# Four samples written out in a row, on two sets of semaphores in turn

## The chip, the cores and the metric

The kernel runs on one core of a Trainium2 chip. The metric is device time in microseconds. Three runs of the kernel before took 4151.75, 4159.27 and 4176.27 us, so its median is 4159.27 us. The profile is one further execution.

## The reference

Four samples (B = 4) of 512 tokens with 512 features pass through four layers, each fed by the one before; the samples do not touch each other.

```python
x = _L0_xattn_ref(x, ctx, mask0, ...)         # attention to ctx, 32 query heads on 8 key heads, add, layernorm
x = _L1_xattn_ref(x, ctx, mask1, mask2, ...)  # self attention, attention to ctx, MLP with gelu (512 -> 2048 -> 512)
x = _L2_xattn_ref(x, ctx, ...)                # RWKV layer: token shift, mixing, linear recurrence over 512 steps, FFN
x = _L3_xattn_ref(x, ctx, ...)                # a second RWKV layer with other weights
```

All is float32. In an attention, `scores = q @ k.T * scale`, the mask is applied, then `softmax(scores) @ v` and an output projection. In an RWKV layer the step is `out = r . (u * a + s)`, `s = a + w * s` with `a = k v`, for 32 heads of 16 by 16.

## The kernel before, in words

The program is written by hand for each engine: TensorE (PE), VectorE (DVE), ScalarE (ACT), GpSimd (POOL) and SyncE (SP, which issues all DMAs) each have their own list of instructions, and only semaphores order them against each other. `build` writes all of it. A class `Signal` holds one semaphore and a counter: `reach(label)` adds one increment and notes its number, `when(label)` gives the semaphore and the number to wait for. `build` is traced twice, so that the numbers are known the second time. DMA loads have semaphores of their own (`LOADS`), and the three slots of the weight ring have `w0` to `w2`.

The order of the work is this. A first block loads five small constants (L227 to L235). A second block (L237) sets `minus_half` on POOL (L240), with an increment of `x_stored`, while DVE scales three vectors (L246). A third block (L1573) issues the first loads: weights `w0`, `ctxT`, `srcT`, `w1`, `maskA`, `w2` (L1568, L1571) and `maskB` (L1578). A block ends with a barrier of all engines: each drains and then passes event semaphores.

Then comes a loop over the samples, `nc.Fori(0, samples)` at L1580, a loop of the hardware: its body stands once in memory and is branched back to. The body holds two blocks. In the first (L1581) POOL alone clears 21 semaphores (L1587): all signals, and the loads other than those that run ahead. In the second (L1589) the whole sample is computed. Since the semaphores start again from zero, each sample waits for the same numbers. PE's waits for weights count from zero too; the semaphores of loads that run ahead (`AHEAD`) are cleared by SP just before their load.

```python
        with nc.Fori(0, samples) as b:
            with nc.Block() as block:
                @block.gpsimd
                def _(pool):
                    for n, s in sems.items():
                        if n not in AHEAD + ['mask1_in', 'x_stored']:
                            nc.gpsimd.sem_clear(s)
```

At the start of a sample (layer 0), PE makes the keys (`pe_k`) and first queries (`pe_q`) through `to_T` (L369), the values through `to_N` (L379), then the other queries, and then the scores (L534). ACT copies a key or query tile out and rounds it to a high part (L624, L629), POOL subtracts to get the low part (`klo`, `lo`, L637), and SP copies high and low parts into stacks for the scores (`sp_stack`, L587). POOL's first instruction of a sample clears `v0` (L1707, a memset), which DVE fills with the values and a bias from `rows` (L702). SP's first instructions are the load of `rows` and, after a wait for `x_stored` (the store of the last sample's output), the load of `x` (both L1748).

At the end of a sample, the second RWKV layer ends with its FFN on PE (three matmuls for each product of high and low parts, L358 or L349), DVE multiplies and adds to `x` (L1336, L1339), and SP stores `x` to `out` (L1801). Before that SP has already issued the loads of the next sample's `ctxT`, `maskA`, `srcT` and its first three weight blocks (`ahead`, L1563).

In each RWKV layer PE has runs of very small matmuls: L966 (`v_blocks`, `k_tok`) and L984 (`pairs`, `rT`), each a run of 128 weight loads and 128 matmuls, four runs of each in a layer, so eight of each in a sample. L924 and L931 follow L966.

Of the kernel before, what the change touches and what calls it, by code (L numbers as in the profile page):

```python
# [23 lines left out]
WSLOTS = 3  # L24
# [50 lines left out]
class Ring:  # L75
# [10 lines left out]
    def bank(self, *label):  # L86
# [3 lines left out]
SIGNALS = ['tile_ready', 'scores_ready', 'context_ready', 'mlp_ready', 'fresh_ready',  # L90
           'act_emptied', 'dve_emptied', 'exp_done', 'act_done', 'scores_taken', 'dve_done', 'inverse_done',
           'pool_done', 'normalised']
LOADS = ['x_in', 'xT_in', 'ctx_in', 'rows_in', 'mask0_in', 'mask1_in', 'mask2_in', 's0_in', 'mixers_in', 'stack0', 'stack1', 'x_stored']

def build(nc, a, known, samples=B):
# [4 lines left out]
    def place(name, shape, offset, dt=F32):  # L101
        n = 1
        for s in shape[1:]:
            n *= s
        assert base + offset + 4 * n <= top, (name, offset + 4 * n)
        return nc.alloc_sbuf_tensor_at(name, shape, dt, offset=base + offset), offset + -(-4 * n // 32) * 32
# [9 lines left out]
    khi0, _ = place('khi0', [P, L], at - 4 * C * L, F32R)  # L116
    klo0, _ = place('klo0', [P, L], at - 4 * (C - 1) * L, F32R)
# [16 lines left out]
    v0, _ = place('v0', [P, C, 8, 32], at - 8192)  # L134
    oT, at = place('oT', [P, C, L], at)
    probs, at = place('probs', [P, PSLOTS, C, L], at)
    xn, _ = place('xn', [P, C, H], at - 4 * PSLOTS * C * L)
    pT, at = place('pT', [P, 4, C, L], at)

    hidden, _ = place('hidden', [P, C, L], at - 4 * (4 + PSLOTS - 1) * C * L)  # L140
    hidden_hi, _ = place('hidden_hi', [P, 2, C, L], at - 4 * 4 * C * L, F32R)
    hidden_lo, _ = place('hidden_lo', [P, 2, C, L], at - 4 * 2 * C * L, F32R)
    mlp_w, _ = place('mlp_w', [P, 2, 2, C * H], at, F32R)
# [13 lines left out]
    xn2, _ = place('xn2', [P, C, H], at - 16 * C * L)  # L157
# [5 lines left out]
    act_lo, _ = place('act_lo', [P, 4, C, L], low_z - 16 * C * L, F32R)  # L163
# [13 lines left out]
    mixers3, _ = place('mixers3', [96, 5 * H], at)  # L177
# [15 lines left out]
    mixers2, _ = place('mixers2', [96, 5 * H], low_z - 12 * C * L)  # L193
# [12 lines left out]
    yn, _ = place('yn', [P, C, L], top_common)  # L206
# [4 lines left out]
    recT, _ = place('recT', [P, C, L], low_z - 16 * C * L)  # L211

    with ExitStack() as stack:
        ps = stack.enter_context(nc.psum_tensor('ps', [P, 8, 512], F32))
        sems = {n: stack.enter_context(nc.semaphore(n)) for n in SIGNALS + LOADS + [f'w{i}' for i in range(WSLOTS)]}
        setup_in = stack.enter_context(nc.semaphore('setup_in'))
        sig = {n: Signal(sems[n], (known or {}).get(n)) for n in SIGNALS}
        ring = Ring((known or {}).get('ring'))
# [8 lines left out]
        with nc.Block() as block:  # L227
            @block.sync
            def _(sp):
                sp.dma_start(cols[:, :], a['cols']).then_inc(setup_in, 16)  # L230
                sp.dma_start(ident[:, :], a['ident']).then_inc(setup_in, 16)
                sp.dma_start(head_sum[:, :], a['head_sum']).then_inc(setup_in, 16)
                sp.dma_start(centre[:, :], a['centre']).then_inc(setup_in, 16)
                sp.dma_start(masks[:, :], a['masks']).then_inc(setup_in, 16)
                sp.wait_ge(setup_in, 16 * 5)  # L235

        with nc.Block() as block:  # L237
            @block.gpsimd
            def _(pool):
                pool.memset(minus_half[:, :], -0.5).then_inc(sems['x_stored'], 16)  # L240

            @block.vector
            def _(dve):

                for k, (n, s) in enumerate((('bq0', 0.25), ('bq1', 32.0 ** -0.5), ('bq2', 32.0 ** -0.5))):
                    dve.tensor_scalar(scaled[:, k * C:(k + 1) * C], cols[:, COL[n]:COL[n] + C], s, None, ALU.mult)  # L246
# [24 lines left out]
        loaded = [WSLOTS]  # L271
# [359 lines left out]
        last_split = {}  # L631
# [148 lines left out]
        def pool_bias(pool, t, row, before):  # L780

            for tc in range(C):
                before(pool, tc)
                nc.gpsimd.tensor_tensor(x[:, tc, :], x[:, tc, :], rows[:, row, :], ALU.add)\
                    .then_inc(*pool_done.reach('biased', t, tc))

        def pool_attention(pool, A):
            t = A.tag
            if A.shared:
                pool_split(pool, A, 'k', 0)  # L790
            for g in range(4 if A.shared else 2):
                pool_split(pool, A, 'q', g)
                if t == 1:
                    pool_split(pool, A, 'k', g)
            for n in range(1, A.heads + 1):
                g, i = divmod(n - 1, 4)
                if not A.shared and g + 2 < A.groups:
                    if i == 1:
                        pool_split(pool, A, 'q', g + 2)
                    if i == 2:  # L800
                        pool_split(pool, A, 'k', g + 2)
                for qc in range(C):
                    pool.wait_ge(*S['inverse_done'].when(t, n - 1, qc // 2))
                    p = probs[:, (n - 1) % PSLOTS, qc, :]
                    nc.gpsimd.tensor_scalar(p, p, row_inv[:, (n - 1) % PSLOTS, qc:qc + 1], 1.0, ALU.mult, ALU.mult)\  # L805
                        .then_inc(*S['normalised'].reach(t, n - 1, qc))
# [751 lines left out]

        AHEAD = ['ctx_in', 'mask0_in', 'xT_in'] + [f'w{n}' for n in range(WSLOTS)]

        def ahead(sp, name, index, clear=True):  # L1563
            if clear:
                sp.sem_clear(sems[name])
# [11 lines left out]
                    ahead(sp, name, 0, clear=False)  # L1577
                sp.dma_start(maskB[:, :, :], a['mask1'].rearrange('(c p) t -> p c t', p=P)).then_inc(sems['mask1_in'], 16)  # L1578

        with nc.Fori(0, samples) as b:  # L1580
            with nc.Block() as block:  # L1581
                @block.gpsimd
                def _(pool):

                    for n, s in sems.items():
                        if n not in AHEAD + ['mask1_in', 'x_stored']:
                            nc.gpsimd.sem_clear(s)  # L1587

            with nc.Block() as block:  # L1589
                @block.tensor  # L1590
# [113 lines left out]
                @block.gpsimd  # L1704
                def _(pool):

                    nc.gpsimd.memset(v0[:, :, :, :], 0.0).then_inc(*pool_done.reach('v0', 'clear'))  # L1707
                    pool_attention(pool, A0)
                    pool.wait_ge(sems['x_in'], 16)
                    pool.wait_ge(sems['rows_in'], 16)  # L1710
                    pool_bias(pool, 0, A0.rowbo, lambda e, tc: None)
                    pool_norm(pool, 'ln0', 1e-6, (0, 1))
                    for tc in range(C):
                        pool.wait_ge(*dve_done.when('gamma', tc))
                        nc.gpsimd.tensor_tensor(x[:, tc, :], xn[:, tc, :], rows[:, 3, :], ALU.add)\
                            .then_inc(*pool_done.reach('x0', tc))
                        if tc + 2 < C:
                            pool_norm(pool, 'ln0', 1e-6, (tc + 2,))
                    pool_norm(pool, 'ln1', 1e-5)
                    pool_neg(pool, A1)  # L1720
                    pool.wait_ge(sems['rows_in'], 32)
                    pool_bias(pool, 1, A1.rowbo, lambda e, tc: e.wait_ge(*dve_done.when('xn', 'ln1', tc)))
                    pool_attention(pool, A1)
                    pool_norm(pool, 'ln2', 1e-5)
                    pool_split(pool, A2, 'k', 0)
                    pool_split(pool, A2, 'k', 1)
                    pool_neg(pool, A2)
                    pool_bias(pool, 2, A2.rowbo, lambda e, tc: e.wait_ge(*dve_done.when('xn', 'ln2', tc)))
                    pool_attention(pool, A2)
                    pool_w(pool, 'up_0')  # L1730
                    pool_norm(pool, 'ln3', 1e-5)
                    pool.wait_ge(sems['rows_in'], 48)
                    pool_w(pool, 'up_1')
                    pool_bias(pool, 'mlp', 0, lambda e, tc: e.wait_ge(*dve_done.when('xn', 'ln3', tc)))
                    for name in MLP_ORDER[2:]:
                        pool_w(pool, name)
                    pool.wait_ge(*act_done.when('mix_w', 2))
                    pool.wait_ge(*pool_done.when('wlo', 'down_3'))
                    nc.gpsimd.tensor_tensor(mix_w2[64:96, :], mixers2[64:96, :], mix_w2[64:96, :].bitcast(F32), ALU.subtract)\
                        .then_inc(*pool_done.reach('mix_w', 2))  # L1740
                    pool.wait_ge(*pool_done.when('mix_w', 2))
                    for l in (2, 3):
                        pool_rwkv(pool, l)
# [59 lines left out]
        with nc.Block() as block:  # L1803
            @block.sync
            def _(sp):
                for name in AHEAD + ['x_stored']:
                    sp.wait_ge(sems[name], 16)
# [94 lines left out]
```

## Time and profile before

| | |
|---|---|
| median of three runs | 4159.27 us (4151.75 to 4176.27) |
| the profiled execution | 4193.48 us |
| its span | 4191.6 us |
| mean granted clock of PE | 0.953 |
| PE matmul busy | 3721.5 us, 89% of the span, 24448 instructions |
| DVE, ACT, POOL busy | 63%, 51%, 39% |
| releases into the four samples' blocks | 13.4, 1062.1, 2099.6, 3148.2 us |

Times in the trace are microseconds from the start of the span; the duration of one instruction is given in ns in the views by line. An engine's name with a q (PEldq, POOLq, SPq) marks an instruction that its sequencer handles alone: a branch, a drain, a semaphore. "Idle before <- X" names what ended a wait; "issue" means that the profile shows nothing that the engine waited for. The granted clock of PE has two levels in this trace, 1.2 and 2.4 GHz.

### The profile page before, as it was taken

Reading aid. Unit: us, or ns where it says so; the run is one execution under the profiler, and the core shown is the slowest. Engines: PE = TensorE matmul, PEld = TensorE weight load, DVE = VectorE, ACT = ScalarE, POOL = GpSimd, SP = SyncE. Lnnn points to the kernel's source line nnn. Section 1 sums busy time; section 2 is a strip of 40 time slices with the busy share of each in tenths; the row PEclk is TensorE's granted clock in tenths of the full one; section 3 lists DMA queues with packets and bytes.
Section 4 is the critical chain, followed back from the end, with each engine's and each line's share of the span. In section 5 each row is a group of like instructions: output and inputs, shape, how many; then the busy total and the mean of one; then the engine's idle time right before and its main releaser. Section 6 shows DMA issues by size and latency. Waiting matters only on the chain. (4 is left out here: it accounts for less than half of the span.)

```text
span 4191.6 us, 66406 instructions
## 1 busy us (share of the span) xinstructions
PE 3721.5 (89%) x24448; PEld 2264.1 (54%) x24448; DVE 2621.2 (63%) x5691; ACT 2149.2 (51%) x4272; POOL 1650.0 (39%) x1849
## 2 busy tenths in 40 slices
PE   7988899898888889989888898998988889899898
PEld 4544575646554456555554545655555444565555
DVE  5765746766576574676667656457666765645766
ACT  5755743434666573343375757334337575733433
POOL 4554442232454454223155445422315544542221
PEclk9999999999999999999999999999999999999999
DMA  4032220202204122110221322111022132210102
GB/s 137 15 100 68 78 80 32 70 21 101 75 15 121 52 82 70 42 60 32 101 69 37 97 63 76 66 39 60 32 101 69 37 98 64 78 68 34 60 32 101
DMA packets 94558, 276.11 MB, mean 66 GB/s; under 512 B 25472, under 2 KB 25984, under 8 KB 73088
## 3 DMA queue, kind: packets, MB, share of 16 engines
q1 hardware_dynamic: 94208, 271.58, 20.1%
q8 instruction: 202, 3.31, 0.3%
q14 instruction: 148, 1.21, 0.1%
HBM read 201.24 MB, written 4.19 MB: 49 GB/s over the span
## 5 line engine op out<-in xcount | busy, mean ns | idle before, releaser
L805 POOL TENSOR_SCALAR probs<-probs,row_inv 128x512 f32<-128x512 f32 x1024 | 694.3, 695 | 639.0 <-DVE row_inv L720 639.0
L664 ACT ACTIVATE probs<-probs,row_max 128x512 f32<-128x512 f32 x1024 | 733.3, 725 | 132.6 <-DVE row_max L736 131.2
L559 PE MATMUL ps<-ident,probs 128*128 128x128 f32 x4096 | 603.3, 288 | 176.9 <-ACT pT L658 150.5
L559 PEld LDWEIGHTS ps<-ident,probs 128*128 128x128 f32 x4096 | 473.9, 145 | 386.5 <-ACT pT L658 215.3
L658 ACT ACTIVATE pT<-ps 128x512 f32<-128x512 f32 x768 | 430.0, 602 | 107.9 <-PE ps L559 107.4
L369 PE MATMUL ps<-mix,wring 128*128 128x512 f32 x1024 | 471.0, 596 | 2.9 <-DMA wring<-in_blocks_dram 2.9
L534 PE MATMUL ps<-kstack,qstack 96*128 96x512 f32 (+1 forms) x1024 | 379.2, 465 | 16.8 <-DMA qstack<-hi 7.2
L736 DVE CUSTOM_DVE_ANT_0 probs<-ps,maskA 128x512 f32<-128x512 f32 x512 | 329.2, 681 | 43.9 <-PE ps L534 43.9
L736 DVE CUSTOM_DVE_ANT_0 probs<-ps,neg 128x512 f32<-128x512 f32 x512 | 340.5, 685 | 8.8
L369 PEld LDWEIGHTS ps<-mix,wring 128*128 128x128 f32 x1024 | 191.3, 190 | 198.0 <-issue 178.6
L1535 POOL TENSOR_TENSOR hinv<-hvar,minus_half 128x32 f32<-128x32 f32 x24 | 146.2, 6092 | 364.5 <-DVE hvar L1255 364.5
L550 PE MATMUL ps<-pT,v 128*32 128x512 f32 x2048 | 243.9, 598 | 0.0
L369 PE MATMUL ps<-srcT,wring 128*128 128x512 f32 x512 | 240.1, 613 | 0.2
L534 PEld LDWEIGHTS ps<-kstack,qstack 96*128 96x128 f32 (+1 forms) x1024 | 176.2, 193 | 109.9 <-issue 43.6
L409 POOL TENSOR_SCALAR varep<-moments 128x1 f32<-128x1 f32 x128 | 42.9, 335 | 481.7 <-DVE moments L388 480.7
L329 POOL TENSOR_TENSOR mlp_w<-wring,mlp_w 128x2048 fp32r<-128x2048 f32 x32 | 149.7, 4678 | 191.2 <-ACT mlp_w L324 191.2
L750 DVE COPY pT<-ps 128x512 f32<-128x512 f32 x256 | 168.3, 686 | 74.1 <-PE ps L559 72.5
L421 PE MATMUL ps<-ident,xn 128*128 128x128 f32 x448 | 101.0, 376 | 126.6 <-DVE xn L392 126.1
L664 ACT ACTIVATION_READ_ACCUMULATOR probs<-probs,row_max 128x1 f32 x1024 | 205.3, 201 | 0.0
L1689 DVE TENSOR_TENSOR hidden_lo<-hidden,hidden_hi 128x512 fp32r<-128x512 f32 x64 | 94.2, 1496 | 168.7 <-ACT hidden_hi L1656 168.7
L1510 POOL TENSOR_TENSOR mix<-mix,xa 128x512 f32<-128x512 f32 x104 | 118.5, 1159 | 173.6 <-DVE mix L1126 124.5
L743 DVE TENSOR_TENSOR ps<-ps,maskA 128x1024 f32<-128x1024 f32 x128 | 156.5, 1222 | 23.5 <-PE ps L534 23.5
(177 smaller groups left out, 7033.2 us busy)
## 6 DMA issues: line engine op xcount, KB each, us to landing
wring<-in_blocks_dram SPq DMA_DIRECT2D x151, 1024.0 KB, 5.0
qstack<-hi SPq DMA_DIRECT2D x256, 64.0 KB, 2.0
kstack<-hi SPq DMA_DIRECT2D x256, 64.0 KB, 2.0
maskA<-in_mask_dram SPq DMA_DIRECT2D x9, 1024.0 KB, 7.7
rows<-in_rows_dram SPq DMA_DIRECT2D x8, 1024.0 KB, 4.6
qstack<-hi SPq DMA_DIRECT2D x256, 32.0 KB, 2.0
qstack<-lo SPq DMA_DIRECT2D x128, 64.0 KB, 2.0
kstack<-lo SPq DMA_DIRECT2D x128, 64.0 KB, 2.0
```

Of the source, the lines that this page charges most:

```text
L329: nc.gpsimd.tensor_tensor(low, weights(name), high.bitcast(F32), ALU.subtract).then_inc(*pool_done.reach('wlo', name))
L369: m = nc.tensor.matmul(tile, w[:, base_ + fc * H + oc * P:base_ + fc * H + (oc + 1) * P], src[:, fc, :], start=(fc == 0), stop=(fc == C - 1))
L534: nc.tensor.matmul(ps[:, qc, :], qstack[0:A.kt, g % 2, i, qc * P:(qc + 1) * P], kstack[0:A.kt, g % 2, 0 if A.shared else i, :], start=True ...
L550: ins = nc.tensor.matmul(ps[32 * h:32 * h + 32, OBANK, :], lhs, pT[:, h, kc, :], start=(kc == 0 and first), stop=(kc == C - 1 and final))
L559: ins = nc.tensor.transpose(tile[:, qc * P:(qc + 1) * P], probs[:, m % PSLOTS, qc, kc * P:(kc + 1) * P], ident[:, :])
L658: nc.scalar.activation(pT[:, m % 4, kc, :], ps[:, ring.bank('pT', t, m, kc), :], ACT.Copy)\
L664: nc.scalar.activation(p, p, ACT.Exp, bias=row_max[:, n % PSLOTS, qc:qc + 1], scale=-1.0, accum_out=row_sum[:, n % PSLOTS, qc:qc + 1]).the ...
L736: nc.vector.tensor_tensor_reduce(out=probs[:, s, qc, :], in0=ps[:, qc, :], in1=other, scale=-1.0, scalar=3.0e38, op0=ALU.add, op1=ALU.min, ...
L743: nc.vector.tensor_tensor(ps[:, two, :], ps[:, two, :], A.mask[:, two, :], ALU.mult)\
L750: nc.vector.tensor_copy(pT[:, m % 4, kc, :], ps[:, ring.bank('pT', t, m, kc), :])\
L805: nc.gpsimd.tensor_scalar(p, p, row_inv[:, (n - 1) % PSLOTS, qc:qc + 1], 1.0, ALU.mult, ALU.mult)\
L1535: nc.gpsimd.tensor_tensor(hinv[:, :, :], hvar[:, :, :], minus_half[:, :].rearrange('p (a b) -> p a b', b=HEADS), ALU.pow).then_inc(*pool_d ...
```

## The change

The hardware loop becomes a Python loop: the body of a sample is written four times into the program, with `b` a plain number. There are two sets of the 21 semaphores. Sample `b` uses set `b % 2`; the `Signal` objects are pointed at that set and their counters are reset, as are the ring's labels and `last_split`. The block that cleared the semaphores is gone. Both sets are cleared once, by POOL, in the second block of the program, ahead of `minus_half`. In samples 1 to 3 POOL clears the set that the sample before used, behind the memset of `v0`. `AHEAD`, `mask1_in` and `x_stored` stay single semaphores.

```diff
@@ -212,7 +212,12 @@
-        sems = {n: stack.enter_context(nc.semaphore(n)) for n in SIGNALS + LOADS + [f'w{i}' for i in range(WSLOTS)]}
+        AHEAD = ['ctx_in', 'mask0_in', 'xT_in'] + [f'w{n}' for n in range(WSLOTS)]
+        KEPT = AHEAD + ['mask1_in', 'x_stored']
+        sems = {n: stack.enter_context(nc.semaphore(n)) for n in KEPT}
+
+        by_parity = [{n: stack.enter_context(nc.semaphore(f'{n}_{p}')) for n in SIGNALS + LOADS if n not in KEPT} for p in range(2)]
+        sems.update(by_parity[0])
@@ -237,6 +242,9 @@
             @block.gpsimd
             def _(pool):
+                for p in range(2):
+                    for s in by_parity[p].values():
+                        nc.gpsimd.sem_clear(s)
                 pool.memset(minus_half[:, :], -0.5).then_inc(sems['x_stored'], 16)
@@ -1577,14 +1583,13 @@
-        with nc.Fori(0, samples) as b:
-            with nc.Block() as block:
-                @block.gpsimd
-                def _(pool):
-
-                    for n, s in sems.items():
-                        if n not in AHEAD + ['mask1_in', 'x_stored']:
-                            nc.gpsimd.sem_clear(s)
+        for b in range(samples):
+            sems.update(by_parity[b % 2])
+            for n, s in sig.items():
+                s.sem, s.count, s.marks = by_parity[b % 2][n], 0, {}
+            ring.labels.clear()
+            last_split.clear()
+            loaded[0] = WSLOTS
 
             with nc.Block() as block:
                 @block.tensor
@@ -1705,6 +1710,9 @@
                     nc.gpsimd.memset(v0[:, :, :, :], 0.0).then_inc(*pool_done.reach('v0', 'clear'))
+                    if b > 0:
+                        for s in by_parity[(b + 1) % 2].values():
+                            nc.gpsimd.sem_clear(s)
                     pool_attention(pool, A0)
```

## Rows read from the trace of the kernel before

**Rows 1.** The page: span, and the queue that fetches TensorE's instructions.
```profile
span 4191.6 us, 66406 instructions
...
q8 instruction: 202, 3.31, 0.3%
```

**Rows 2.** Waits of TensorE, whole trace: total us, times, longest us.
```profile
PE ps L369 <- PEq L1581: 45.3, 4, 13.7
...
PE ps L966 <- issue: 29.3, 15, 2.7
```

**Rows 3.** Sequencer instructions, 2088 to 2101: ns min/median/max, first and last start.
```profile
L1589 SPq EVENT_SEMAPHORE  x1: 17/17/17, 2091.7 to 2091.7; - x1
...
L1580 PEldq COMPARE_BRANCH  x1: 5565/5565/5565, 2092.0 to 2092.0; - x1
...
L1587 POOLq EVENT_SEMAPHORE_RANGE_CLEAR  x21: 44/44/44, 2097.9 to 2099.3; - x21
...
L1581 SPq EVENT_SEMAPHORE  x1: 17/17/17, 2099.6 to 2099.6; - x1
```

**Rows 4.** The same, whole trace, then 1050 to 1064, then 3136 to 3149.
```profile
L1589 SPq EVENT_SEMAPHORE  x4: 17/17/17, 1054.0 to 4187.6; - x4
...
L1581 SPq EVENT_SEMAPHORE  x4: 17/17/17, 13.4 to 3148.2; - x4
...
L1581 SPq EVENT_SEMAPHORE  x1: 17/17/17, 1062.1 to 1062.1; - x1
...
L1589 SPq EVENT_SEMAPHORE  x1: 17/17/17, 3140.3 to 3140.3; - x1
```

**Rows 5.** Timeline of the start (start us, us, what), and L1587 there.
```profile
4.92 0.12 POOL L240 MEMSET minus_half<- 128x32 f32 x1 [4.49 <-POOLq L227]
...
5.53 0.33 SPq L1568 DMA_DIRECT2D wring<-in_blocks_dram  x1
...
29.13 0.88 DVE L702 TENSOR_TENSOR v<-ps,rows 128x64 f32<-128x64 f32 x6 [23.86 <-DMA rows<-in_rows_dram]
...
L1587 POOLq EVENT_SEMAPHORE_RANGE_CLEAR  x21: 44/44/48, 11.7 to 13.1; - x21
```

**Rows 6.** Timeline of sample 2's start; last, landing of the stores of L1801.
```profile
2099.86 5.71 PE L369 MATMUL ps<-ctxT,wring 128*128 128x512 f32 x8 [10.49 <-PEq L1581]
...
2105.41 3.60 PE L369 MATMUL ps<-srcT,wring 128*128 128x512 f32 x8
...
2107.04 1.27 POOL L637 TENSOR_TENSOR klo<-split,khi 128x512 fp32r<-128x512 f32 x1 [6.42 <-ACT khi L629]
...
2109.99 0.35 DVE L702 TENSOR_TENSOR v<-ps,rows 128x64 f32<-128x64 f32 x2 [19.08 <-PE ps L379]
...
DMA to landing us min/median/max: 4.3/5.0/5.2
```

**Rows 7.** Timeline of TensorE about three L966 runs.
```profile
684.58 1.44 PE L966 MATMUL ps<-v_blocks,k_tok 32*32 32x128 f32 x92
687.86 1.29 PE L966 MATMUL ps<-v_blocks,k_tok 32*32 32x128 f32 x36 [1.84 <-issue]
689.09 3.78 PE L924 MATMUL ps<-rk,head_sum 128*128 128x512 f32 x4
...
1726.66 1.89 PE L966 MATMUL ps<-v_blocks,k_tok 32*32 32x128 f32 x128
1728.48 1.98 PE L924 MATMUL ps<-rk,head_sum 128*128 128x512 f32 x4
...
2800.28 0.70 PE L966 MATMUL ps<-v_blocks,k_tok 32*32 32x128 f32 x20 [2.67 <-issue]
2800.91 3.36 PE L924 MATMUL ps<-rk,head_sum 128*128 128x512 f32 x4
```

**Rows 8.** Waits of TensorE in sample 1, then in sample 2.
```profile
PE ps L966 <- issue: 3.9, 2, 2.7
...
PE ps L966 <- issue: 10.3, 5, 2.7
```

More of the change, by code:

```diff
@@ L1556, in pool_rwkv @@
             pool_w(pool, f'fv_{l}')
-        AHEAD = ['ctx_in', 'mask0_in', 'xT_in'] + [f'w{n}' for n in range(WSLOTS)]
         def ahead(sp, name, index, clear=True):
```

## The prediction

> **What bounds the kernel now.** I read the page first. The span is 4191.6 us [rows 1], so the profiled execution (4193.5 us with what lies around the span) stands 34.2 us, 0.8%, above the median of 4159.3 us; the three runs themselves lie 24.5 us apart. What I count below is in the profiled execution's own microseconds, and the sum is then taken off the median. About 0.5% (20.8 us) is what a measurement of this kernel can tell from no change.
>
> The waits of TensorE (PE) come second. The longest single ones are at the head of a sample: 45.3 us in 4 waits [rows 2]. A smaller entry matters too: 29.3 us in 15 waits for "issue", all inside L966. Third, the sequencers' own instructions about one boundary [rows 3]. All engines are released from sample 1's block at 2091.7; PE's COMPARE_BRANCH of the loop lasts 5565 ns, though the decision is trivial; 21 semaphore clears run on POOL from 2097.9 to 2099.3; the release into sample 2's block is at 2099.6. Nothing is computed in those 7.9 us. The other two boundaries give 8.1 and 7.9 us (1054.0 to 1062.1, 3140.3 to 3148.2) [rows 4]. Fourth, the start of the trace and of a sample [rows 5, 6], and fifth the L966 stalls [rows 7, 8].
>
> **The change, part by part.**
>
> (A) The back edge and the clearing block go, the barrier at the end of a sample's block stays. Taken out is release to release: 8.1 + 7.9 + 7.9 = 23.9 us [rows 3, 4]. What is now exposed is nothing new: the first instructions start 0.1 to 0.2 us after a release, as before. Bounds: all 23.9, or only the 21 clears and a barrier if each entry into a new block costs a fetch as the back edge does (rival 3).
> The trace's 5.6 us branch decides against a printed figure: the Trainium skill, Advanced Engine Details and Errata, Control Flow Timing, puts a compare-and-branch at about 108 ns, and by that (A) would save some 7 us instead of 23.9. The same notes explain the difference under Runtime: NRT & Kernel Launch, Instruction fetch mechanics: a taken branch to a page that is not loaded waits for its fetch; the row agrees.
>
> (B) At the head, POOL now issues 42 clears ahead of its memset, whose end the first load waits for through a barrier (memset at 4.92, first load at 5.53 [rows 5]). 21 clears started over 1.4 us (11.7 to 13.1 [rows 5]), 0.07 us each, so 42 take 2.9; 0.2 us of it hides beside VectorE's three multiplications, leaving 2.7. The clearing block of sample 0 (1.8 us) goes, but sample 0 is paced by the loads, not by the block: VectorE waits 23.86 us for `rows` until 29.13 [rows 5], behind 7 MB that are issued first. Later loads move it by the full 2.7. Lower bound 2.7 - 1.8 = 0.9 if the block paced it. I take +2.7.
>
> (C) The 21 clears of a finished set run on POOL after the memset of v0: 1.5 us. POOL's next work, klo, starts 7.4 us after the release (2107.04 against 2099.6 [rows 6, 3]); cost 0, with 7.4 - 1.5 = 5.9 us of cover for the memset alone. If the cover were gone, klo would hold the first stack DMAs and so the first scores. On SP, the x load waits for the store of `out` to land, 4.3 to 5.2 us after its issue [rows 6]; until now that passed in the gap. It now blocks SP for up to 4 us, but what stands behind it, the first stack copy, waits for klo (8.7 us after the release). Cost 0; cover 4 us. `rows` shares the DMA queues with that store, and VectorE wants it 10.3 us after the release (2109.99 [rows 6]); cost 0.
>
> (D) PE's clock. PE now idles 10.49 us and its next eight matmuls take 5.71 us where the following eight take 3.60 [rows 6]: 2.1 us lost, 6.3 in three boundaries. With 7.9 us less the idle time is 2.6 us. The nearest rows for such a gap: after 2.67 us of idling four L924 matmuls took 3.36 us, after 1.84 us 3.78 us, against 1.98 us with no gap before them [rows 7]. So a short gap does not spare the clock: 1.4 to 1.8 us lost in these groups alone, perhaps 3 with what follows. I price three boundaries at 3 x 2.2 = 6.6; against 6.3 before this is +0.3. Bounds: 3 x 3 - 6.3 = +2.7, and -6.3 if the clock holds.
>
> (E) Where the code's pages end. The page counts 202 fetches, 3.31 MB, on one instruction queue [rows 1]: 16.4 KB each. Over the trace's records I count 12,590 PE instructions in a sample, so 4 x 12,590 / 202 gives 249, that is pages of 256. L966 is a run of 128 weight loads and 128 matmuls, one page's worth, done in 1.9 us when nothing stops it (1726.66 [rows 7]). The stalls cut it only after 92, 106, 108, 122 or 124 pairs (92 are done at 684.58; at 2800.28 20 of 128 are left [rows 7]); counted from a sample's first PE instruction each of them comes at the remainder 183 of 256, in every sample. In a loop every sample has the same addresses. The same place does not always stall (no stall at 1726.66), but no L966 run with its page end before pair 92 did, and none of the 32 runs of L984 (page ends at pairs 38 to 82).
> Written out, a sample is 4 PE instructions shorter, 12,586 = 49 x 256 + 42. The page end moves 21 pairs forward in each sample. Sample 0 stays as it is but for two pairs (3 stalls, as before); sample 1 keeps two L966 runs above pair 100; samples 2 and 3 none, though five L984 runs there get their page end at pairs 105 to 126. The eight L966 runs of a sample have five such places and stalled 15 times in 20; at that rate seven places give 5, so I expect 8 stalls instead of 15.
> Price: sample 1 had 3.9 us of stalls and took 1029.6 us from release to release, sample 2 had 10.3 us and took 1040.7 [rows 8, 3, 4]. That is 11.1 us for 6.4 us of stalls, 1.7 each, as the slowed clock comes on top; all 29.3 us cost some 50. 7 of 15 stalls would be 23 us of the profiled execution. The timed runs are 34.2 us quicker than it; if that is stalls not met, 16 us are left there, and 7/15 of them are 7 us. Bounds 0 and -23; I take -7, by the timed runs, since those are predicted.
> The Trainium skill, Runtime: NRT & Kernel Launch, Instruction fetch mechanics, calls the crossing of a page mostly hidden. By that (E) would be 0 and the sum 7 us smaller; the 2.7 us stalls in L966 speak against it.
>
> Sum: -23.9 + 2.7 + 0 + 0.3 - 7 = -27.9, so 4159.3 - 27.9 = 4131 us. On the profiled execution's own 4193.5 us, with 23 for (E), it would be 4150.
>
> **Rivals.**
> 1. The pages move and nothing is won: as many stalls, elsewhere. Then -20.9, 4138 us, on the bound of what can be told. For it: which stall is met varies from sample to sample. Against: the depth at which they fall does not.
> 2. Stalls nearly all go, in the timed runs too: -20.9 - 23, 4115 us. For it: samples 2 and 3 lose all their places. Against: the timed runs seem to have fewer to lose.
> 3. The gap stays though the loop goes: each engine leaves its block by a branch, and if the next block's code isn't loaded, some 5.9 us return per boundary: -20.9 + 17.7 = -3, 4156 us. Against: PE leaves its block now after 12,000 instructions, and its drain and semaphore go on at once (release 2091.7, loop's branch 2092.0 [rows 3]), so code behind a block lies next to it.
> 4. Slower: the new page ends fall badly. 64 runs (L966 and L984) each hold one page end; 15 stall now. From 15 + 20.9 / 3.3 = 21 stalls on (23 us for 7 is 3.3 each) the gain is gone; at 30 it is -20.9 + 50 = +29, 4188 us. Against: L984's 32 runs never stalled; for: none had its end so deep.
>
> **How the numbers follow.** Forecast 0.48 (own range 4118 to 4146), rival 1 0.23, rival 2 0.13, rival 3 0.09, rival 4 0.07. The likeliest is 4131 us. The range, 4110 to 4154, takes in rivals 1 and 2 nearly whole, the bounds of (B) and (D), and some 8 us by which a median of few runs moves; it leaves out rivals 3 in half and 4. Faster by over 0.5% (under 4138.5): 0.40 + 0.10 + 0.12 = 0.62. Slower by over 0.5%: 0.05 of rival 4. Within: 0.33.
>
> **What would show it.** Right: one barrier between two samples, under 0.5 us from release to the first instructions, no long COMPARE_BRANCH; the first load at 8.2 instead of 5.53; PE idle 2.6 us at a boundary and still slow in its first matmuls; the L966 stalls at changed depths, about 8 in number. Wrong: a gap of over 2 us after a release; klo or the first stack copy later than 9 us after it; PE waiting for `rows` in samples 1 to 3; 20 stalls or more, or L984 among them.

## The result, and the profile after

| | before | after |
|---|---|---|
| median of the timed runs, us | 4159.27 (7 runs, 4148.68 to 4176.27) | 4140.54 (7 runs, 4128.82 to 4149.18) |
| profiled execution, us | 4193.48 | 4149.18 |
| span, us | 4191.6 | 4147.4 |
| mean granted TensorE clock | 0.953 | 0.954 |

The ratio after to before is 0.9925 (95% interval 0.9903 to 0.9948), about 31 us by the ratio and 19 us by the two medians. A second comparison gave 0.9923 (0.9897 to 0.9948), 32 us by the ratio and 33 us by its medians. The ratios are what is used below. One execution of a later run (the loop with hint and slot 148) took 13,694 us at a granted clock of 0.507 and is left out of its ratio. The forecast was 4131 us in a range of 4110 to 4154, faster: direction and range held. The changed kernel's profiled execution is its slowest of seven, and that of before is slower than all of its timed ones, so the 44 us between the two spans are more than the change is worth.

A helper's line of before stands 8 lines further down after: L966 is now L974, L984 is L992, L369 is L377, L534 is L542, L559 is L567, L637 is L645, L664 is L672, L1801 is L1809.

First the page's span and its instruction queue, which answer to [rows 1]:

```profile
span 4147.4 us, 66284 instructions
...
q8 instruction: 196, 3.21, 0.3%
```

Then TensorE's waits over the whole trace (us in total, times, longest), which answer to [rows 2]:

```profile
PE ps L377 <- DMA ctxT<-in_ctxT_dram: 16.4, 1, 16.4
...
PE ps L542 <- DVE row_max L744: 10.4, 22, 1.5
...
PE ps L974 <- issue: 9.7, 5, 3.0
...
PE ps L377 <- PEq L1594: 7.7, 3, 2.6
...
PE ps L992 <- issue: 5.7, 3, 2.2
...
PE ps L377 <- issue: 1.6, 1, 1.6
```

The wait at the head of a sample was 45.3 us in four; it is now 7.7 us in three, and the first sample's 16.4 us go to the context's load. "issue" was 29.3 us in 15 waits, all in L966. It is 17.0 us in 9: five in L974, three in L992 (the old L984), where there was none before, and one in L377.

Third the sequencers' instructions at L1594, where a sample's block ends (ns min/median/max, first and last start), then the clears; they answer to [rows 3] and [rows 4]:

```profile
L1594 SPq EVENT_SEMAPHORE  x4: 17/17/17, 1057.7 to 4143.3; - x4
...
L1594 PEldq COMPARE_BRANCH  x4: 163/166/179, 1051.2 to 4136.8; - x4
...
L1715 POOLq EVENT_SEMAPHORE_RANGE_CLEAR  x63: 44/44/44, 1057.8 to 3114.5; - x63
...
L247 POOLq EVENT_SEMAPHORE_RANGE_CLEAR  x42: 44/44/48, 4.8 to 7.7; - x42
```

There is one barrier per sample, no branch of 5.6 us, and the 63 clears run after a release, behind the memset of v0. Fourth the timeline at the end of sample 0, which answers to [rows 6] (start us, us, what):

```profile
1056.98 0.40 SPq L1809 DMA_DIRECT2D out_dram<-x  x1
1057.79 0.33 SPq L1756 DMA_DIRECT2D rows<-in_rows_dram  x1
1057.80 0.95 POOL L1712 MEMSET v<- 128x1024 f32 x1 [17.34 <-POOLq L1594]
1057.98 5.37 PE L377 MATMUL ps<-ctxT,wring 128*128 128x512 f32 x8 [2.58 <-PEq L1594]
1062.45 0.38 SPq L1756 DMA_DIRECT2D x<-in_x_dram  x1
...
1064.82 1.26 POOL L645 TENSOR_TENSOR klo<-split,khi 128x512 fp32r<-128x512 f32 x1 [6.07 <-ACT khi L637]
1066.11 1.15 SPq L595 DMA_DIRECT2D kstack<-khi  x2
...
1067.77 0.36 DVE L710 TENSOR_TENSOR v<-ps,rows 128x64 f32<-128x64 f32 x2 [10.81 <-PE ps L387]
```

This is the clean part. From the store of a finished sample to the next sample's first load there were 8.93, 8.73 and 8.68 us (1053.23 to 1062.16, 2090.94 to 2099.67, 3139.55 to 3148.23). Now there are 0.81, 0.80 and 0.80. The load of x waits for the store (1062.45), 3.7 us ahead of the first stack copy that stands behind it, so it holds nothing up. POOL's klo waits for ACT and not for the clears.

Last, the start, which answers to [rows 5]:

```profile
7.80 0.12 POOL L248 MEMSET minus_half<- 128x32 f32 x1 [7.38 <-issue]
8.24 0.33 SPq L1574 DMA_DIRECT2D wring<-in_blocks_dram  x1
...
16.38 6.15 PE L377 MATMUL ps<-ctxT,wring 128*128 128x512 f32 x8 [16.38 <-DMA ctxT<-in_ctxT_dram]
...
32.21 0.88 DVE L710 TENSOR_TENSOR v<-ps,rows 128x64 f32<-128x64 f32 x6 [27.03 <-DMA rows<-in_rows_dram]
```

VectorE gets `rows` at 32.21 instead of 29.13, 3.1 us later.

Two theories then had to be told apart. **Theory:** the gain has two sources, the boundary (some 20 us, fixed in every execution) and the shift of the page ends of TensorE's code (7 us or more). **Rival:** the boundary alone, and the stalls that changed place are worth nothing. The experiments undo or move one of the two. Ratios are to the kernel before, run beside them on the same chip; its median was 4171 to 4176 us there.

### The profile page after: what moved, and what is told of

Read it like the earlier page. It is cut to its first block and busy times, and to the rows that moved or that the text cites. A ratio compares the mean times of both kernels' runs of the same rounds, so it can differ in the third digit from the quotient of the medians.

```text
span 4147.4 us, 66284 instructions
## 1 busy us (share of the span) xinstructions
PE 3717.0 (90%) x24448; PEld 2274.3 (55%) x24448; DVE 2623.6 (63%) x5691; ACT 2149.6 (52%) x4272; POOL 1650.5 (40%) x1849
## 5 line engine op out<-in xcount | busy, mean ns | idle before, releaser
L672 ACT ACTIVATE probs<-probs,row_max 128x512 f32<-128x512 f32 x1024 | 733.6, 726 | 129.4 <-DVE row_max L744 128.3
L567 PE MATMUL ps<-ident,probs 128*128 128x128 f32 x4096 | 608.9, 290 | 173.4 <-ACT pT L666 147.2
L567 PEld LDWEIGHTS ps<-ident,probs 128*128 128x128 f32 x4096 | 478.8, 147 | 383.7 <-ACT pT L666 210.7
L377 PE MATMUL ps<-mix,wring 128*128 128x512 f32 x1024 | 477.5, 603 | 5.0 <-DMA wring<-in_blocks_dram 3.4
L542 PE MATMUL ps<-kstack,qstack 96*128 96x512 f32 (+1 forms) x1024 | 380.2, 466 | 19.0 <-DVE row_max L744 10.4
L377 PEld LDWEIGHTS ps<-mix,wring 128*128 128x128 f32 x1024 | 193.9, 192 | 204.2 <-issue 184.8
L377 PE MATMUL ps<-srcT,wring 128*128 128x512 f32 x512 | 238.0, 608 | 0.2
L542 PEld LDWEIGHTS ps<-kstack,qstack 96*128 96x128 f32 (+1 forms) x1024 | 176.6, 193 | 111.5 <-DVE row_max L744 46.5
L672 ACT ACTIVATION_READ_ACCUMULATOR probs<-probs,row_max 128x1 f32 x1024 | 206.6, 202 | 0.0
```

The lines of the kernel that those rows point to most:

```text
L377: m = nc.tensor.matmul(tile, w[:, base_ + fc * H + oc * P:base_ + fc * H + (oc + 1) * P], src[:, fc, :], start=(fc == 0), stop=(fc == C - 1))
L542: nc.tensor.matmul(ps[:, qc, :], qstack[0:A.kt, g % 2, i, qc * P:(qc + 1) * P], kstack[0:A.kt, g % 2, 0 if A.shared else i, :], start=True ...
L567: ins = nc.tensor.transpose(tile[:, qc * P:(qc + 1) * P], probs[:, m % PSLOTS, qc, kc * P:(kc + 1) * P], ident[:, :])
L672: nc.scalar.activation(p, p, ACT.Exp, bias=row_max[:, n % PSLOTS, qc:qc + 1], scale=-1.0, accum_out=row_sum[:, n % PSLOTS, qc:qc + 1]).the ...
```

## Experiments on the loop

**The loop with its back edge hinted.**

```diff
-        with nc.Fori(0, samples) as b:
+        with nc.Fori(0, samples, hint_back_edge=True) as b:
```

Measured: ratio 0.998 (0.9958 to 1.0001). The loop's own instructions on TensorE's queue:

```profile
L1580 PEldq BRANCH_PREFETCH_HINT  x4: 31/31/45, 11.7 to 3118.3; - x4
...
L1580 PEldq COMPARE_BRANCH  x4: 95/372/382, 1051.7 to 4150.1; - x4
```

and the same of the kernel before:

```profile
L1580 PEldq COMPARE_BRANCH  x4: 85/5594/5653, 1054.2 to 4187.9; - x4
```

A hint ahead of it takes the taken branch from 5.6 us to 0.4 and nothing else was changed, so 5.2 us of its length were the wait for the code it jumps to. The Trainium skill, Runtime: NRT & Kernel Launch, Instruction fetch mechanics, states that a taken branch to a page that isn't loaded waits for its fetch; the trace agrees. Store to next load fell to 3.1 to 3.2 us, 17 us in three boundaries. The whole kernel won 8 by the ratio, with an interval from nothing to 17 us; there were 11 stalls in L966 in its profile, 21.1 us.

**The loop's first TensorE instruction at slot 148 of a page.** It stands at slot 72 in the kernel before, and two instructions of TensorE lie between the loop's head and a sample's body, which therefore starts at slot 74. Nothing else changes, so every page end falls 76 instructions earlier in the code.

```diff
-        with nc.Fori(0, samples) as b:
+        with nc.Fori(0, samples, head_slot={mybir.EngineType.PE: 148}) as b:
```

> The kernel before, its loop's first PE instruction put at slot 148 of a page of 256 instead of 72, so that all page ends come 76 instructions earlier: at pairs 30 to 86 in L966 and 0 to 43 in L984. Same instructions otherwise. Theory (a page end deep in a dense run stalls PE, and a us of stall costs 1.7): stalls fall from 15 to 0 or 1; the timed runs gain 16 us (0.4%), the profiled one up to 50. Rival (the stalls' place costs the timed runs nothing, they are an effect of the profile or are hidden): no move, within 4 us.

Measured: ratio 0.9929 (0.9902 to 0.9956), 30 us, with the boundaries untouched. TensorE's waits:

```profile
PE ps L369 <- PEq L1581: 45.7, 4, 13.9
...
PE ps L369 <- issue: 9.1, 7, 2.1
```

No wait is left inside L966. Seven shorter ones appear in L369 (1.3 us each instead of 2.0). So where page ends fall is worth as much as the whole change (0.9925), by one argument to the loop.

**Slot 22.** The same argument with 22.

> The kernel before, its loop's first PE instruction at slot 22, so that 8 of a sample's 16 dense runs (4 of L966, 4 of L984) have their page end behind pair 92 instead of 5. Theory: some 24 stalls instead of 15, in L984 too, which had none; timed runs slower by 9/15 of 16 us, 10 us (0.24%), up to 30 us if the stalls cost as much in timed runs as in the profile. Rival (only the place in L966 matters, not the depth): fewer stalls, 12, and no loss.

Measured: ratio 0.9973 (0.9955 to 0.9991), 11 us faster and not slower. Its profile has five waits in L966 (7.9 us together), four in L924 (5.6 us) and four in L931 (2.3 us). L984 has none, though its runs have page ends 96 to 107 pairs deep. The theory expected 24 stalls and a loss of 10 us, so the count of places by depth is refuted as a price for this slot.

**Both.**

```diff
-        with nc.Fori(0, samples) as b:
+        with nc.Fori(0, samples, hint_back_edge=True, head_slot={mybir.EngineType.PE: 148}) as b:
```

> The kernel before, still a loop, with the back edge hinted and PE's loop head at slot 148. Theory: the two parts add. Slot 148 alone gave 29 us (ratio 0.9929) and the hint alone 8 us of the 17 that its branches got shorter (0.998), so the ratio is between 0.9909 (sum of the two) and 0.9888 (if the hint's other 9 us had gone to other page ends), and PE's branch takes 0.4 us instead of 5.6. Rival (the two overlap: what slot 148 won was in part the clock's rest at the boundary): 0.9929 again.

Measured: ratio 0.9888 (0.9863 to 0.9912), at the further end of what the theory gave. By the two ratios (0.9929 and 0.9888) the hint is worth 17 us here, as much as the gaps between two samples got shorter. It was 8 us alone; each ratio is known to about 10 us, so these two values do not differ clearly.

## Experiments on the row of samples

**Page ends put back to where the loop has them.** TensorE's body starts at slot 74 in every sample, as in the loop; the file of the changed kernel is otherwise the same. The jump over the unused slots costs a little by itself: TensorE's waits at the boundaries are 8.8 us instead of 7.7.

```diff
                 @block.tensor
                 def _(pe):
+                    pe.addr_align(256, offset=74, max_nops=0)
                     pe_attention(pe, A0)
```

> The kernel after, with each sample's first PE instruction put back at the slot that it had in the loop (74), all else as after: it takes back only the moved page ends. One branch over unused slots comes into each sample. Theory: stalls back at about 15, the time 7 us (0.17%) above the kernel after, so about 22 to 24 us under the kernel before by the ratio; if the profile's price holds, 23 us above the kernel after. Rival (the page ends don't matter): as the kernel after, 0.9925 of before.

Measured: ratio 0.996 (0.994 to 0.998), 17 us under the kernel before and 15 us above the changed one, where 7 were expected. Its profile has 8 stalls and not the expected 15, all in L974 and all at places where the loop stalled. The boundary's gain stays and the rest of the change's goes.

**Slot 150 in the same line**, the counterpart of the loop's 148.

> The changed kernel with PE's block body in every sample starting at instruction slot 150 of a page of 256, nothing else. Theory (page ends set where PE waits for code): slot 148 left no wait inside L966 or L984 of the loop, so this leaves none inside L974 and L992, which took 15.4 us (9.7 and 5.7) in the profile after. The ratio to the kernel before should be 0.989 (0.9925 of the change less 15.4 of 4149), about 28 us under the one with slot 74 (0.996). Rival 1 (a stall that goes comes back in other lines, as L924 and L931 got 7.9 us with slot 22): ratio at the changed kernel's 0.9925. Rival 2 (the matmuls run denser and the granted clock takes the time back): no waits, more low-clock time than 387 us, ratio at 0.9925 too.

Measured: ratio 0.9864 (0.9839 to 0.9888), 4119.6 us. TensorE's waits at the boundary and for "issue":

```profile
PE ps L377 <- PEq L1594: 8.8, 3, 2.9
PE ps L377 <- issue: 7.9, 6, 1.9
```

None in L974 or L992. The expected gain was 15.4 us (0.9925 to 0.989), and 25 came by the ratios. Rival 1 is right in part: six waits came into L377, in runs of longer matmuls. Rival 2 is refuted by the time.

**The three again beside each other, with a slot meant to be the worst.** The changed kernel, slot 74, slot 150, and slot 4, all on one chip.

> The changed kernel itself once more, so that it, slots 74, 150 and 4 stand against one kernel before on one chip. Ratio 0.9925 as measured. Theory (a page end that falls 87 to 127 pairs into a run of 128 pairs costs PE 1.2 to 1.7 us on average over executions, whether or not it shows as a wait in the one profiled): this kernel has 15 such ends, so it stands 18 to 25 us above slot 150. Its profile need not show the same 8 waits again.

> Slot 74 again (page ends in every sample as in the loop): 24 page ends 87 to 127 pairs into a run. Theory: 9 ends more than the changed kernel, 11 to 15 us above it and 29 to 41 us above slot 150. Rival (only the waits that a profile shows count, 8 in both): equal to the changed kernel.

> Slot 150 again, no page end in the last third of a run: ratio 0.9864 as before, no wait inside L974 or L992.

> PE's body at slot 4, the worst that the count gives: 10 page ends per sample fall 87 to 127 pairs into a run (4 in L974, 6 in L992), 40 in all. Theory: 40 x 1.2 to 1.7 = 48 to 68 us above slot 150, a ratio of 0.998 to 1.003: what the unrolling won is all lost again. Rival 1 (L992 stalls less, as slot 22 of the loop had no wait there): only the 16 ends in L974 count, 19 to 27 us above slot 150, ratio 0.991 to 0.993. Rival 2 (the waits are a chance of the single execution and not of the slot): as slot 74.

| TensorE's body | ratio | 95% | median us | "issue" waits in the profile, us |
|---|---|---|---|---|
| slot 74 | 0.9955 | 0.9939 to 0.9971 | 4154.0 | 14.9 (7) |
| as changed | 0.9923 | 0.9897 to 0.9948 | 4141.2 | 15.1 (8) |
| slot 4 | 0.9908 | 0.9883 to 0.9932 | 4136.9 | 11.8 (7) |
| slot 150 | 0.9870 | 0.9843 to 0.9898 | 4122.3 | 8.2 (6), all in L377 |

The first, second and fourth line repeat what they gave before to 0.0006; from the changed kernel to slot 150 it is 22 us by the ratios and 19 by the medians. Slot 74 and the changed kernel came as the theory of 1.2 to 1.7 us per deep page end had them. Ten executions of slot 74 took 4148.9 to 4159.6 us and six of the changed kernel 4134.4 to 4149.4, on one chip, so the shifted page ends are worth something. Slot 4 was to be the worst by my count and is the second best: 16 us above slot 150 by the ratios instead of 48 to 68, close to rival 1 (19 to 27). Its waits:

```profile
PE ps L974 <- issue: 11.8, 7, 2.0
PE ps L377 <- PEq L1594: 9.1, 3, 3.0
```

and one of the stalled runs in its timeline:

```profile
3772.26 1.88 PE L974 MATMUL ps<-v_blocks,k_tok 32*32 32x128 f32 x127
3776.15 0.41 PE L974 MATMUL ps<-v_blocks,k_tok 32*32 32x128 f32 x1 [2.01 <-issue]
```

All seven come after 124 or 127 pairs, in the second run of a layer, where there are eight such places. The page ends at 103 and 105 pairs of the layer's first run stalled in none of eight cases, and the 24 places in L992 in none. In the changed kernel L992 does stall, at 105, 107 and 126. One of them:

```profile
3764.84 1.71 PE L992 MATMUL ps<-pairs,rT 32*32 32x128 f32 x107 [0.42 <-ACT pairs L1448]
3768.49 0.47 PE L992 MATMUL ps<-pairs,rT 32*32 32x128 f32 x21 [1.93 <-issue]
```

So depth in the run isn't the whole condition. Rival 1 is right that L992 doesn't stall here, but all stalls lie in eight of its 16 places in L974. Depth finds places where a stall can be, and many of them never have one. What else counts wasn't isolated.

**One set of semaphores again, in a row.** Slot 150, the second set gone, a block for the clears between two samples.

```diff
+            if b > 0:
+                with nc.Block() as block:
+                    @block.gpsimd
+                    def _(pool):
+                        for s in by_parity[0].values():
+                            nc.gpsimd.sem_clear(s)
...
                     nc.gpsimd.memset(v0[:, :, :, :], 0.0).then_inc(*pool_done.reach('v0', 'clear'))
-                    if b > 0:
-                        for s in by_parity[(b + 1) % 2].values():
-                            nc.gpsimd.sem_clear(s)
```

> The samples in a row with slot 150 as in row_slot150, but on one set of 21 semaphores, which POOL clears in a block of its own between two samples (three more barriers, no taken branch). Theory (the loop's 8 us between releases were mostly PE's fetch on the taken branch, 5.6 us): the block costs what was left once the branch was hinted, 2.3 us from one release to the next, so 7 us in all, a ratio 0.0017 above row_slot150 and some 2.3 us between two releases in the trace. Rival (every entry into a new block costs a fetch, hinted or not): 5 us or more per block, 15 us in all, 0.0036 above row_slot150.

Measured: ratio 0.9893 (0.987 to 0.9916), so 12 us above slot 150, with intervals that overlap. By the time alone the rival (0.0036) is as near as the theory (0.0017); the trace decides. The timeline of its first boundary:

```profile
1043.86 0.40 SPq L1814 DMA_DIRECT2D out_dram<-x  x1
1046.41 0.33 SPq L1761 DMA_DIRECT2D rows<-in_rows_dram  x1
1046.42 0.95 POOL L1720 MEMSET v<- 128x1024 f32 x1 [18.70 <-POOLq L1595]
...
1046.96 6.34 PE L377 MATMUL ps<-ctxT,wring 128*128 128x512 f32 x8 [4.68 <-PEq L1595]
```

Store to next load is 2.55 us instead of 0.81, so the clears and their barrier cost 1.7 us per boundary, 5.2 in all; the rival's 5 us per block is refuted. The second set of semaphores therefore accounts for some 5 of the change's 24 us at the boundaries, and the code written out for the other 19. With one set there are also 21 clears fewer at the head, and the load of `rows` is issued 1.2 us earlier (13.11 instead of 14.32). Against that, the eight matmuls behind the wait of 4.68 us took 6.34, 6.39 and 5.37 us, at granted clocks of 0.58, 0.57 and 0.68, where slot 150 has 5.37 each time. Some 6 of the 12 us stay unexplained.

**The three leaks closed.** Slot 150, the 42 clears in the first block, and an Exp of one column at the head of ACT's block, written to a column `scrap` that nobody reads.

```diff
         with nc.Block() as block:
+            @block.gpsimd
+            def _(pool):
+                for p in range(2):
+                    for s in by_parity[p].values():
+                        nc.gpsimd.sem_clear(s)
             @block.sync
             def _(sp):
                 sp.dma_start(cols[:, :], a['cols']).then_inc(setup_in, 16)
...
             def _(pool):
-                for p in range(2):
-                    for s in by_parity[p].values():
-                        nc.gpsimd.sem_clear(s)
                 pool.memset(minus_half[:, :], -0.5).then_inc(sems['x_stored'], 16)
...
+                    nc.scalar.activation(scrap[:, 0:1], cols[:, 0:1], ACT.Exp)
                     act_attention(act, A0)
```

> row_slot150 with two more edits: the 42 clears go into the first block, where POOL has nothing to do while the constants load, and ACT begins each sample with one Exp of a column that nobody reads, so that its table is loaded while PE does the first products. Theory: the first load of the main part comes 2.7 us earlier, the ACT_TABLE_LOAD falls into the first 10 us of each sample and the first transposes come some 1.3 us earlier after the first scores in three samples: 2.7 + 3 x 1.3 = 6.6 us, a ratio 0.0016 under row_slot150. Rival for the head (the constants' loads land later than POOL is done, so nothing is hidden or POOL is the one waited for): 0 us of the 2.7. Rival for the table (the scores' own products hold the next step, not row_max): 0 of the 3.9.

Measured: 4114.3 us, ratio 0.9849 (0.9824 to 0.9873), the fastest of all: 6 us under slot 150 against 6.6 expected, in intervals that overlap. The profile shows both parts, which the time alone couldn't. Its start:

```profile
4.83 0.12 POOL L252 MEMSET minus_half<- 128x32 f32 x1 [4.40 <-POOLq L233]
4.88 0.31 DVE L258 TENSOR_SCALAR scaled<-cols 128x4 f32<-128x4 f32 x3 [4.88 <-PEq L233]
5.45 0.33 SPq L1578 DMA_DIRECT2D wring<-in_blocks_dram  x1
```

The clears hide beside the constants' loads, the first load is issued at 5.45 instead of 8.18 (slot 150), and VectorE has `rows` at 29.16. The table is the next section's. Two of this profile's three boundaries also have the faster first matmuls (3.67 us instead of 5.37), 3.4 us that neither edit made.

## Why the prediction was right, and by how much each step

**(A), the boundary, -23.9: right.** 8.1, 7.9 and 7.9 us went, to the tenth. Rival 3 (a fetch at each block's entry) is refuted: TensorE's first matmul starts 0.2 us after `rows` is issued, as before. As for the 108 ns that the Trainium skill, Advanced Engine Details and Errata, Control Flow Timing, gives for a compare-and-branch: of the loop's four only the shortest comes near it (85 ns before, 95 hinted); the others took 5.6 us unhinted and 0.37 hinted, and those at the end of a block after the change 163 to 179 ns.

**(B), the clears at the head, +2.7: right.** The first load came 2.7 us later (8.24 for 5.53), the first scores 3.0 us (46.85 for 43.84).

**(C), cost 0: right.** None of its covers was used up: klo starts 7.0 us after the load of `rows` is issued and waits for ACT, and SP, held by the store until 1062.45, issues the first stack copy at 1066.11.

**(D), the clock, +0.3: right in this profile, wrong as a rule.** TensorE idles 2.58 us at each boundary and its next eight matmuls take 5.37 us at a granted clock of 0.68 (a mix of the levels of 1.2 and 2.4 GHz). Before it idled 10.5 to 10.7 us, and they took 5.64, 5.71 and 5.38 us at 0.65, 0.64 and 0.68. That is -0.6 in three boundaries. But the second profile of the same kernel shows, at its first boundary:

```profile
1050.50 3.67 PE L377 MATMUL ps<-ctxT,wring 128*128 128x512 f32 x8 [2.58 <-PEq L1594]
```

The same idle time, and a granted clock of 1.00. Two of its three boundaries are like that, which makes -4.0 there. Over the eight profiles with a wait of 2.6 to 3.0 us the clock was 0.68 behind 18 boundaries and 1.00 behind 6; behind none of the 18 waits of 4.7 us or more (six profiles) was it over 0.72. So the short gap does spare the clock at times, and the prediction had that only as its bound. What decides it isn't known.

**A term that was missing: ACT's table, +4.2.** In the loop ACT loads its table at the head of every sample, in L624, while it has nothing to do. In the row samples 1 to 3 have no load there, and the first one stands at the first Exp, L672; both profiles have 40 table loads in all, so these three only moved. Presumably the tables left loaded by the sample before serve the first functions, and not Exp. ACT's table loads before (busy us, mean ns, idle before):

```profile
L624 ACT ACT_TABLE_LOAD x4 | 5.1, 1283 | 70.6 <-PEq L1581 70.6
```

and after, with the place of the first:

```profile
L672 ACT ACT_TABLE_LOAD x3 | 3.8, 1283 | 0.1
L632 ACT ACT_TABLE_LOAD x1 | 1.3, 1283 | 14.8 <-PEq L1579 14.8
...
1082.06 1.28 ACT L672 ACT_TABLE_LOAD   x1
```

Now it stands between the first maximum and the first Exp, where VectorE's next maximum and TensorE wait behind it. After:

```profile
1080.59 1.19 PE L542 MATMUL ps<-kstack,qstack 48*128 48x512 f32 x4
...
1085.80 0.50 PE L542 MATMUL ps<-kstack,qstack 48*128 48x512 f32 x1 [1.49 <-DVE row_max L744]
...
1089.16 1.12 PE L567 MATMUL ps<-ident,probs 128*128 128x128 f32 x4
```

With the Exp at the head of ACT's block:

```profile
1060.12 1.19 PE L546 MATMUL ps<-kstack,qstack 48*128 48x512 f32 x4
...
1064.03 0.50 PE L546 MATMUL ps<-kstack,qstack 48*128 48x512 f32 x1 [0.18 <-DVE row_max L748]
...
1067.31 1.97 PE L571 MATMUL ps<-ident,probs 128*128 128x128 f32 x8
```

From the first scores to the first transposes it is 8.57 us after, 7.19 with the early Exp, and 7.19 before (1085.23 to 1092.42). That is 1.4 us in three samples, and 8.57 or 8.58 in each of the three. The prediction looked only at instructions that the source issues, and no line of the source asks for this one: it is put in by the compiler. That a compiler which sees the samples in a row knows more of what is loaded than in a loop is my explanation; the runs show only the moved place and its price.

**(E), the page ends, -7: right in sign and in the number of stalls, too small in worth.** Eight stalls in L974 and L992 were forecast, and eight came (seven in the second profile), but not at the listed places: sample 0 had four and then one instead of three, and stalls came after 89 and 91 pairs, which the rule had as harmless. Three of the eight are in L992, the old L984. The prediction contradicts itself there: it counts five such runs among its seven places, and yet lists a stall in L984 as a sign of being wrong. The rate behind the count, 15 of 20 places, came from one execution; the same 20 places stalled 8 and 7 times in the two profiles of slot 74, so that the total was met is luck. What the shift is worth comes from slot 74, which undoes it: 0.996 and 0.9955 against 0.9925 and 0.9923, or 13 to 15 us of 4172, about 1 of it for the jump over the unused slots. The step that was mis-sized is the one that scaled the stalls down for the timed runs ("if that is stalls not met, 16 us are left there"). Slot 148 shows that it took too little: with L966's stalls gone the timed loop is 30 us faster, where the prediction left all of them 16 us.

The sum by measured terms: -23.9 + 3.0 + 4.2 - 0.6 = -17.3 without the page ends, against 17 and 19 us that slot 74 won; with 14 for the page ends -31, as measured (31 and 32 by the two ratios). Forecast was -27.9. So two errors of opposite sign, a missing +4 and a -7 that should have been about -14, cancelled in part, and that much of the agreement is luck. The 4150 us that the prediction gave for the profiled execution were met too (4149.18), with -23 for the page ends where the other terms leave -27. The sum itself is known to a few us only: (D) is -0.6 in one profile and -4.0 in the other.

Rival 1 (nothing from the page ends) would have been slot 74's 17 to 19 us; two comparisons speak against it, though the intervals overlap a little. Rival 4 is refuted. Rival 2 (nearly all stalls gone) isn't what the change does, but is what slot 150 does with it, and there it gives more than the rival's 44 us: 0.9864, 57 us.

**Still open.** The profiles of slot 74 and of the changed kernel show the same waits for issue (14.9 to 15.9 us against 15.1 to 17.0), though the timed runs differ by 13 us. The profiled executions aren't typical: of slot 74 the second is the fastest of its ten, of the changed kernel the first is the slowest of its seven. Stalls do differ between executions of one kernel: the two profiles of slot 74 share only three of their 8 and 7 stalled places. Whether that explains the difference is open, since no timed execution shows its stalls. The spread of the timed runs does not settle it: 41 us for the kernel before (29 runs), 28 us for slot 74 (12 runs) but 11 us the second time (10 runs), 16 and 22 us for slot 150 (5 and 6 runs), and 11 us for slot 4 (6 runs), which has the most deep ends.

## What to carry to other kernels

A loop's boundary is priced from the trace by what lies between the last store and the next load. If it holds a branch of microseconds, try a hint on the back edge and the slot of the loop's head first: the two together (0.9888) gave at least as much as writing the loop out (0.9925; the intervals overlap a little), with the loop's body still once in the program. The row with a chosen slot (0.9864) stands ahead of both by its ratio. When code is written out or moved, all page ends behind it move, so a few tens of microseconds can come or go that have nothing to do with the edit; run a second slot before the edit is praised or blamed. And look for what the compiler put at the head of an iteration, where it was free: a table load goes to its first use, which may be on the path.

## What the runs showed of the hardware

A taken back edge cost TensorE's queue 5.6 us, and 0.37 us with a hint of 31 ns given ahead. A clear of a semaphore took 44 ns and came every 0.07 us on POOL (42 from 4.8 to 7.7 us). In dense runs of 128 weight loads and 128 small matmuls, TensorE stood still at some of the ends of a page of 256 instructions, for 0.2 to 3.0 us (15 times and 29.3 us in the profile before, 2.0 us on average). The Trainium skill, Runtime: NRT & Kernel Launch, Instruction fetch mechanics, calls such crossings mostly hidden. Most are here, too (202 pages were fetched and 15 stalls seen), but where the ends fall is worth 20 to 30 us (0.5 to 0.7%) in this kernel: 30 in the loop (slot 148 against 72) and some 20 in the row (slot 150 against the natural one). Whether an end stalls depends on more than its depth in the run: slot 4, with the most deep ends of all, was no slower than the natural slots (0.9908 against 0.9923). After a wait of 2.6 to 3.0 us TensorE's granted clock was 0.68 in three cases of four and 1.00 in the fourth; after 4.7 us or more it was never over 0.72.
